# Linear-attention stack: one gelu group per pass on ScalarE, with feed-forward chunks 2 and 3 moved up on TensorE

## The chip, the cores and the metric

One NeuronCore of one Trainium2 chip runs the whole program. The metric is the device time of one execution in microseconds (us); lower is better. The engines work side by side and meet only at semaphores: TensorE (PE in the rows; PEld is its weight loads) multiplies matrices, VectorE (DVE) and ScalarE (ACT) work on tiles, GpSimd (POOL) does small work, and SyncE (SP) issues transfers. Each takes its instructions in the order in which they are written.

## The reference, cut to what matters

The program is a two-block network on 4096 tokens of width 128. The change touches only the attention of the second block, a stack of eight linear-attention layers with a feed-forward each:

```python
for i in range(8):
    residual = x
    Q = elu(einsum('nsd,hdk->nshk', x, Wq[i]) + bq[i]) + 1
    Kf = elu(einsum('nsd,hdk->nshk', x, Wk[i]) + bk[i]) + 1
    V = einsum('nsd,hdk->nshk', x, Wv[i]) + bv[i]
    KV, sumK = sum(Kf * V, axis=1), sum(Kf, axis=1)
    Z = 1.0 / (Q * sumK[:, None] + 1e-06)
    att = (Q * KV[:, None] * Z).reshape(n, s, H * K)
    y = gelu(att @ Wo[i] + bo[i])
    x = layer_norm(y + residual, ln1_s[i], ln1_b[i])
    residual = x
    h = gelu(x @ W1[i] + b1[i])
    h = gelu(h @ W2[i] + b2[i])
    x = layer_norm(h + residual, ln2_s[i], ln2_b[i])
```

There are 16 heads of 64, so Q, Kf and V have 1024 rows per token; the hidden width of the feed-forward is 512. Each layer therefore has three gelus. A unit of 512 tokens has six gelu instructions: one on y, four on the chunks of the hidden layer, and one on the second product.

## The kernel before, in words

The stack (`stack_phase`, L1378) cuts the tokens into eight units of 512 (two images of 256) and takes the 64 pairs of layer and unit one after the other. It is a software pipeline, unrolled by `run` (L1459): pass t does the first part of unit t, and later parts of units t-1 to t-4. In the code A, B, C, Dn and E say whether the unit with lag 0, 1, 2, 3 or 4 exists. From pass 4 to pass 63 all five do; from pass 3 on there is a unit with lag 3. Every engine has a `step` function that writes its part of a pass in a fixed order by hand, and the engines are joined by counting semaphores alone. Nothing reorders them.

What one pass does around the change:

- The 1024 rows of K, Q and V are made in four quarters of two 128-row chunks. `biases` (L1514) writes the bias rows of K and Q of a quarter into PSUM (it waits until VectorE has taken the quarter before: k_ready and q_ready). `keys`, `queries` and `values` (L1533 to L1545) then run three matmuls of 512 columns per chunk, because each weight and each input is split into a high and a low part. `values` makes one chunk at a time in a single bank, and waits until VectorE has drained the chunk before (v_drained).
- ScalarE takes exp of each quarter (`exp_keys` L1699, `exp_queries` L1703), VectorE makes the feature maps from it (`feature_k` L1826, `feature_q` L1865), and multiplies and sums keys with values (`values` L1837, "drain the values").
- For the unit with lag 1, ScalarE makes 1/(Q sumK) by a log (`log_z` L1707) and an exp (`exp_z` L1720); VectorE multiplies it in (`attention` L1872), quarter by quarter; and TensorE projects each quarter with Wo (`project` L1547), which waits for att_ready. Quarter 0 is done in the same pass as the quarter-0 and quarter-1 keys of the next unit.
- For the unit with lag 3, `first_feed_forward` (L1558) makes the four hidden chunks. They use two PSUM banks in turn: chunk 2 waits for the gelu of chunk 0 (hid_ready), chunk 3 for the gelu of chunk 1. `first_gelu` (L1688) takes them on ScalarE. `second_feed_forward` (L1570) sums them.
- `turn` (L1580) transposes a 128 x 512 tile by four small matmuls. The normalisations run on VectorE between two turns (`layernorm_stats` L1884, then GpSimd's `rstd_of`, then `normalise` L1893).

ScalarE's functions come in sets: gelu is in one, exp and log are together in another, and to change the set it runs an ACT_TABLE_LOAD. In a pass it now has two groups of gelus. The first has four: the second product's (L1749), chunk 0, y (L1754), chunk 1. Then come a load of the exp and log set (L1762), `exp_z` of quarter 0, and `exp_keys` and `exp_queries` of quarter 1; then a load of the gelu set, the gelus of chunks 2 and 3, and again a load of the exp and log set (L1777), before `log_z` of quarter 1. TensorE's order there is (L1618 to L1645, without the waits of a layer's first pass):

```python
first_feed_forward(t - 3, 1)
biases(t, 1)
values(t, s, 0, 0)
keys(t, s, 1)
queries(t, s, 1)
first_feed_forward(t - 3, 2)
values(t, s, 0, 1)
first_feed_forward(t - 3, 3)
project(t - 1, r, 0)
turn(m0, y2, c["z2_turned"])
values(t, s, 1, 0)
biases(t, 2)
queries(t, s, 2)
turn(m1, y1, c["z1_turned"])
keys(t, s, 2)
turn(m0, y2, c["n2_turned"])
```

VectorE's order between the drain of the last values chunk of unit t-1 and its second normalisation is: add y2 and x1; `finish_sums`; drain values (t, 0, 0); `attention` (t-1, 0); `feature_k` (t, 1); drain values (t, 0, 1); `feature_q` (t, 1); `layernorm_stats` of y2; add y1; drain values (t, 1, 0); `normalise` y2.

The last pass of a layer also moves the next layer's weights into place on ScalarE and VectorE (`swap`), and the first pass of the next layer the rest of them.

Of the kernel before, what the change touches and what calls it, by code (L numbers as in the profile page):

```python
# [1377 lines left out]
def stack_phase(nc, sem, d, g):  # L1378
# [10 lines left out]
    with ExitStack() as ctx:  # L1389
# [76 lines left out]
        def active(at, lag):  # L1466

            return 0 <= at - lag < UNITS
# [41 lines left out]
        def _(pe):  # L1510
# [13 lines left out]
            def three_pass(out, kind, chunk, s, first):  # L1524
                cols = slice(chunk * P, (chunk + 1) * P)
                pe.matmul(out, w_hi[:, kind, cols], x_hi[:, s, :], start=first, stop=False, skip_group_check=True)  # L1526
                pe.matmul(out, w_hi[:, kind, cols], x_lo[:, s, :], start=False, stop=False, skip_group_check=True)  # L1527
                return pe.matmul(out, w_lo[:, kind, cols], x_hi[:, s, :], start=False, stop=True, skip_group_check=True)  # L1528

            def weights_ready(u, piece):  # L1530
                pe.wait_ge(c["w_ready"], NS * layer_of(u) + place_of_swap[piece] + 2)

            def keys(t, s, q):  # L1533
                for half in range(2):
                    last = three_pass(k_ps[:, half * UNIT:(half + 1) * UNIT], 0, 2 * q + half, s, False)
                last.then_inc(c["k_filled"], 1)

            def queries(t, s, q):
                for half in range(2):
                    last = three_pass(q_ps[:, half * UNIT:(half + 1) * UNIT], 1, 2 * q + half, s, False)  # L1540
                last.then_inc(c["q_filled"], 1)

            def values(t, s, q, half):
                pe.wait_ge(c["v_drained"], 8 * t + 2 * q + half + 1)
                three_pass(v_ps[:], 2, 2 * q + half, s, True).then_inc(c["v_filled"], 1)  # L1545

            def project(u, s, q):  # L1547

                pe.wait_ge(c["att_ready"], 4 * u + q + 2)
                if q == 0:  # L1550
                    pe.wait_ge(c["y1_ready"], u + 1)
                pe.wait_ge(wo_in[q], 16 * layer_of(u) + 16)
                for chunk in (2 * q, 2 * q + 1):
                    last = pe.matmul(o_ps[:], wo[:, chunk, :], feat_q[:, s, chunk, :], start=(chunk == 0), stop=(chunk == NC - 1),  # L1554
                                     skip_group_check=True)
                last.then_inc(c["o_filled"], 1)

            def first_feed_forward(u, j):  # L1558

                bank, cols = (m1, m0)[j % 2], slice(j * P, (j + 1) * P)  # L1560
                if j == 0:
                    pe.wait_ge(c["x1_split"], u + 2)
                    pe.wait_ge(c["w1_ready"], layer_of(u) + 2)
                else:
                    pe.wait_ge(c["hid_ready"], 4 * u + max(j, 1))
                pe.matmul(bank[:], w1_hi[:, cols], x1_hi[:], start=True, stop=False)
                pe.matmul(bank[:], w1_hi[:, cols], x1_lo[:], start=False, stop=False)
                pe.matmul(bank[:], w1_lo[:, cols], x1_hi[:], start=False, stop=True).then_inc(c["w1_filled"], 1)
# [11 lines left out]
            def turn(bank, y, turned):  # L1580
                for i in range(4):
                    last = pe.transpose(bank[:, i * P:(i + 1) * P], y[:, i * P:(i + 1) * P], ident)  # L1582
                last.then_inc(turned, 1)

            def step(t, at, closing=None, opening=None, second=False):
                s, r = at % 2, 1 - at % 2
                A, B, C, Dn, E = (active(at, k) for k in range(5))
                opens = opening is not None or at == 0
                bias_step = 4 * layer_of(t) + 2
                if C:  # L1590
                    project(t - 2, s, 1)
                if Dn:
                    pe.wait_ge(c["n1_ready"], 4 * (t - 3) + 5)
                    turn(m1, y1, c["n1_turned"])
                if A:
                    if opens:
                        pe.wait_ge(c["b3_ready"], bias_step)
                    biases(t, 0)
                    pe.wait_ge(c["x_split"], t + 2)
                    if opens:  # L1600
                        weights_ready(t, (KEYS, 0))
                    queries(t, s, 0)
                    keys(t, s, 0)
                if B:
                    if second or at == 1:
                        weights_ready(t - 1, (VALUES, 3))
                    values(t - 1, r, 3, 0)
                if Dn:
                    first_feed_forward(t - 3, 0)
                if C:  # L1610
                    project(t - 2, s, 2)
                    project(t - 2, s, 3)
                if B:
                    values(t - 1, r, 3, 1)
                if Dn:
                    if E:
                        pe.wait_ge(c["y2_ready"], t - 4 + 2)
                    first_feed_forward(t - 3, 1)  # L1618
                if A:
                    if opens:  # L1620
                        pe.wait_ge(c["b3_ready"], bias_step + 1)
                    biases(t, 1)
                    if opens:
                        weights_ready(t, (VALUES, 0))
                    values(t, s, 0, 0)
                    keys(t, s, 1)
                    queries(t, s, 1)
                if Dn:
                    first_feed_forward(t - 3, 2)
                if A:  # L1630
                    values(t, s, 0, 1)
                if Dn:
                    first_feed_forward(t - 3, 3)
                if B:
                    project(t - 1, r, 0)
                if E:
                    pe.wait_ge(c["z2_ready"], t - 4 + 2)
                    if Dn:
                        pe.wait_ge(c["hid_ready"], 4 * (t - 3) + 5)
                    turn(m0, y2, c["z2_turned"])  # L1640
                if A:
                    if opens:
                        pe.wait_ge(c["b3_ready"], bias_step + 2)
                        weights_ready(t, (VALUES, 1))
# [3 lines that stand above are left out]
                if C:  # L1648
                    pe.wait_ge(c["z1_ready"], t - 2 + 2)
                    if Dn:  # L1650
                        pe.wait_ge(c["hid_ready"], 4 * (t - 3) + 4)
                    turn(m1, y1, c["z1_turned"])
                if A:
                    keys(t, s, 2)
                if E:
                    pe.wait_ge(c["n2_ready"], 4 * (t - 4) + 5)
                    turn(m0, y2, c["n2_turned"])
                if A:
                    values(t, s, 1, 1)
                if Dn:  # L1660
                    second_feed_forward(t - 3, E)
                if A:
                    if opens:
                        pe.wait_ge(c["b3_ready"], bias_step + 3)
                        weights_ready(t, (VALUES, 2))
                    values(t, s, 2, 0)
                    biases(t, 3)
                    keys(t, s, 3)
                    queries(t, s, 3)
                    values(t, s, 2, 1)  # L1670
# [4 lines left out]
        def _(act):  # L1675
            act.wait_ge(const_in, 32)

            def param(u, k):
                return params[:, bass.ds(layer_of(u), 1), k]
# [8 lines left out]
            def first_gelu(u, j):  # L1688

                act.wait_ge(c["w1_filled"], 4 * u + j + 2)  # L1690
                act.activation(hid[:, j, :], (m1, m0)[j % 2][:], ACT.Gelu_apprx_tanh, bias=param(u, 1 + j)).then_inc(c["hid_ready"], 1)
# [33 lines left out]
            def step(t, at, closing=None, opening=None, second=False):  # L1725
                s, r = at % 2, 1 - at % 2
                A, B, C, Dn, E = (active(at, k) for k in range(5))
# [30 lines left out]
                    swap(opening, VALUES, 3)  # L1758
                if Dn:
                    first_gelu(t - 3, 1)  # L1760
                if A or B:
                    act.preload_act_table_set("natural_log_exp_and_others")  # L1762
                if B:
# [4 lines left out]
                if closing is not None:  # L1768
# [1 line left out]
                    swap(closing, QUERIES, 1)  # L1770
                    act.wait_ge(c["v_filled"], 8 * t + 3)
                    swap(closing, VALUES, 0)
                if Dn:
                    first_gelu(t - 3, 2)
                    first_gelu(t - 3, 3)
                if A or B:
                    act.preload_act_table_set("natural_log_exp_and_others")  # L1777
                if B:
                    log_z(t - 1, r, 1)
                    exp_z(t - 1, 1)  # L1780
# [815 lines left out]
```

## Time and profile before

| What | us |
|---|---|
| Median of 3 runs | 3323.68 |
| Lowest and highest of them | 3323.03, 3341.3 |
| The profiled execution | 3324.58 |
| Its span in the trace | 3322.8 |
| The stack's steady stretch, 1000 to 3000 of the span | granted clock 1.00 |
| From one pass to the next, most passes | 35.1 |
| The last pass of a layer | 38.2 |

The span runs from the first to the last instruction in the trace, and the profiled execution's own time is 1.8 us more. Start times are counted from the start of the span. A row of the timeline gives the start, the busy time, the engine, the line, the operation with the tiles it writes and reads, how many like it are merged in the row, and in brackets how long its engine stood idle before it and which instruction ended the wait. The durations of matmuls overlap: they are pipelined, so that the pitch from start to start is what one costs. The granted clock is 1.00 at 2.4 GHz and 0.50 at 1.2 GHz.

### The profile page before, as it was taken

The numbers are of one execution on the slowest core, as the hardware profiler recorded it, in microseconds if no ns is written. First come the engines' busy times: TensorE is split into PE (matmuls) and PEld (weight loads), VectorE is DVE, ScalarE is ACT, GpSimd is POOL, SyncE is SP. The second block draws the span as 40 slices with busy tenths as digits, with TensorE's granted clock in tenths as the row PEclk, the third lists the DMA queues.
The fourth block names the chain that finished last, engine by engine and source line by source line (L and its number), as shares of the span: only waits on it lengthen the run. The fifth ranks groups of instructions, "written<-read, shape, count | busy, mean of one in ns | idle before, by whom it ended". The sixth has DMA issues, their size and how long they took to land. (4 is left out here: it accounts for less than half of the span.)

```text
span 3322.8 us, 49526 instructions
## 1 busy us (share of the span) xinstructions
PE 3011.6 (91%) x14486; PEld 1989.9 (60%) x14486; DVE 2777.8 (84%) x11011; ACT 2463.9 (74%) x4579; POOL 589.9 (18%) x715
## 2 busy tenths in 40 slices
PE   7999998282799999999999999999999999999779
PEld 5777776271566566566666656666665665666454
DVE  6878786864689999998999998999989999898566
ACT  6878786132578878878888888888888888878535
POOL 0000001276011111111111111111211111111124
PEclk9999998585999999999999999999999999999869
DMA  1000000323000000000000000000000000000000
GB/s 55 1 1 1 0 1 4 110 39 90 1 1 1 7 26 1 3 31 1 1 7 26 1 4 29 1 1 7 26 1 7 26 1 1 7 11 1 1 1 26
DMA packets 35120, 46.39 MB, mean 14 GB/s; under 512 B 5768, under 2 KB 26304, under 8 KB 34880
## 3 DMA queue, kind: packets, MB, share of 16 engines
q1 hardware_dynamic: 29248, 39.47, 3.6%
q0 software_dynamic: 5632, 4.20, 1.0%
q8 instruction: 93, 1.52, 0.2%
q14 instruction: 147, 1.20, 0.1%
HBM read 35.16 MB, written 8.49 MB: 13 GB/s over the span
## 5 line engine op out<-in xcount | busy, mean ns | idle before, releaser
L1880 DVE TENSOR_SCALAR t_feat_q<-t_recip,t_neg_mean 128x256 f32<-128x256 f32 x1024 | 385.5, 438 | 131.4 <-ACT t_recip L1723 131.4
L1554 PE MATMUL t_o_ps<-t_feat_q,t_wo 128*128 128x512 f32 x1024 | 473.0, 595 | 2.7 <-DVE t_feat_q L1880 2.7
L1715 ACT ACTIVATE t_recip<-t_feat_q,t_z_scale 128x256 f32<-128x256 f32 x1024 | 434.7, 498 | 3.5 <-DVE t_feat_q L1880 2.7
L1701 ACT ACTIVATE t_exp_k<-t_k_ps 128x1024 f32<-128x1024 f32 x256 | 259.4, 1013 | 230.2 <-PE t_k_ps L1528 230.2
L1843 DVE CUSTOM_DVE_ANT_0 t_junk<-t_v_ps,t_feat_k 128x256 f32<-128x256 f32 x1024 | 390.3, 418 | 6.1 <-PE t_v_ps L1528 6.0
L1833 DVE SCALAR_TENSOR_TENSOR t_feat_k<-t_exp_k,t_k_ps 128x256 f32<-128x256 f32 x1024 | 368.7, 415 | 21.4 <-ACT t_exp_k L1701 21.4
L1705 ACT ACTIVATE t_exp_q<-t_q_ps 128x1024 f32<-128x1024 f32 x256 | 261.7, 1022 | 96.8 <-PE t_q_ps L1528 94.5
L1869 DVE SCALAR_TENSOR_TENSOR t_feat_q<-t_exp_q,t_q_ps 128x1024 f32<-128x1024 f32 x256 | 312.5, 1221 | 8.8
L2008 POOL TENSOR_TENSOR t_var_eps<-t_moments,t_ln_eps 128x4 f32<-128x4 f32 x128 | 69.2, 540 | 1300.1 <-DVE t_moments L1891 1300.1
L1554 PEld LDWEIGHTS t_o_ps<-t_feat_q,t_wo 128*128 128x128 f32 x1024 | 194.3, 190 | 175.4 <-issue 154.5
L1526 PE MATMUL t_v_ps<-t_x_hi,t_w_hi 128*128 128x512 f32 x512 | 264.4, 516 | 10.1 <-DVE t_sum_kv L1843 9.3
L1723 ACT ACTIVATE t_recip<-t_recip 128x1024 f32<-128x1024 f32 x256 | 269.7, 1054 | 2.7
L1577 PE MATMUL t_m<-t_hid,t_w 128*128 128x512 f32 x512 | 241.1, 615 | 18.4 <-ACT state_t L1785 18.4
L1526 PE MATMUL t_q_ps<-t_x_hi,t_w_hi 128*128 128x512 f32 x512 | 218.1, 426 | 2.5 <-POOL t_x_lo L2015 2.5
L1526 PE MATMUL t_k_ps<-t_x_hi,t_w_hi 128*128 128x512 f32 x512 | 216.9, 424 | 0.0
L1582 PEld LDWEIGHTS t_m<-ident,t_y 128*128 128x128 f32 x1024 | 118.9, 142 | 150.6 <-issue 92.9
L1896 DVE TENSOR_SCALAR t_y<-t_m,t_moments,t_rstd 128x128 f32<-128x128 f32 x512 | 174.3, 400 | 36.4 <-POOL t_rstd L2010 36.4
L1528 PE MATMUL t_k_ps<-t_x_hi,t_w_lo 128*128 128x512 f32 x512 | 204.3, 399 | 0.0
L1528 PE MATMUL t_q_ps<-t_x_hi,t_w_lo 128*128 128x512 f32 x512 | 204.0, 398 | 0.0
L1527 PE MATMUL t_k_ps<-t_x_lo,t_w_hi 128*128 128x512 f32 x512 | 203.7, 398 | 0.0
L1527 PE MATMUL t_q_ps<-t_x_lo,t_w_hi 128*128 128x512 f32 x512 | 203.5, 397 | 0.0
L1527 PE MATMUL t_v_ps<-t_x_lo,t_w_hi 128*128 128x512 f32 x512 | 202.8, 396 | 0.0
(365 smaller groups left out, 7341.2 us busy)
## 6 DMA issues: line engine op xcount, KB each, us to landing
t_raw_w<-in_wq SPq DMA_DIRECT2D x8, 512.0 KB, 3.7
t_raw_w<-in_wk SPq DMA_DIRECT2D x8, 512.0 KB, 4.8
t_raw_w<-in_wv SPq DMA_DIRECT2D x8, 512.0 KB, 5.6
t_wo<-in_wo SPq DMA_DIRECT2D x32, 128.0 KB, 2.2
x<-in_x SPq DMA_DIRECT2D x4, 512.0 KB, 8.4
tokens_dram<-r_hn SPq DMA_DIRECT2D x8, 256.0 KB, 2.3
e_w_raw<-in_fc_w SPq DMA_DIRECT2D x4, 512.0 KB, 4.0
e_w<-in_fc_w SPq DMA_DIRECT2D x4, 512.0 KB, 4.9
```

The source lines that it names most:

```text
L1526: pe.matmul(out, w_hi[:, kind, cols], x_hi[:, s, :], start=first, stop=False, skip_group_check=True)
L1527: pe.matmul(out, w_hi[:, kind, cols], x_lo[:, s, :], start=False, stop=False, skip_group_check=True)
L1528: return pe.matmul(out, w_lo[:, kind, cols], x_hi[:, s, :], start=False, stop=True, skip_group_check=True)
L1554: last = pe.matmul(o_ps[:], wo[:, chunk, :], feat_q[:, s, chunk, :], start=(chunk == 0), stop=(chunk == NC - 1), skip_group_check=True)
L1701: act.activation(exp_k[:], k_ps[:], ACT.Exp, bias=-1.0).then_inc(c["k_exp"], 1)
L1705: act.activation(exp_q[:], q_ps[:], ACT.Exp, bias=-1.0).then_inc(c["q_exp"], 1)
L1715: last = act.activation(recip[:, q % 2, k * UNIT + n * SEQ:k * UNIT + (n + 1) * SEQ], feat_q[:, s, chunk, cols], ACT.Ln, bias=1.0, scale=z ...
L1723: act.activation(recip[:, q % 2, :], recip[:, q % 2, :], ACT.Exp, scale=-1.0).then_inc(c["recip_ready"], 1)
L1833: last = dve.scalar_tensor_tensor(feat_k[:, q % 2, cols], exp_k[:, cols], 1.0, k_ps[:, cols], ALU.min, ALU.max, accum_out=sum_k[:, s, n, 2 ...
L1843: last = dve.tensor_tensor_reduce(junk[:, n, :], v_ps[:, n * SEQ:(n + 1) * SEQ], feat_k[:, q % 2, k * UNIT + n * SEQ:k * UNIT + (n + 1) * ...
L1869: dve.scalar_tensor_tensor(feat_q[:, s, 2 * q:2 * q + 2, :], exp_q[:].rearrange("p (k t) -> p k t", k=2), 1.0, q_ps[:].rearrange("p (k t) ...
L1880: last = dve.tensor_scalar(feat_q[:, s, chunk, cols], recip[:, q % 2, k * UNIT + n * SEQ:k * UNIT + (n + 1) * SEQ], -1.0, neg_mean[:, s, n ...
```

## The change

On TensorE the order inside a pass becomes: values chunk 0, feed-forward chunk 2, keys of quarter 1, feed-forward chunk 3, queries of quarter 1, values chunk 1, projection of quarter 0. On ScalarE the gelus of chunks 2 and 3 follow that of chunk 1 at once, ahead of the load of the exp and log set; their former place, and the second load of that set, are gone. VectorE, GpSimd and SyncE keep their programs. All waits stay attached to the same instructions.

```diff
@@ TensorE's step
                     values(t, s, 0, 0)
-                    keys(t, s, 1)
-                    queries(t, s, 1)
                 if Dn:
                     first_feed_forward(t - 3, 2)
                 if A:
-                    values(t, s, 0, 1)
+                    keys(t, s, 1)
                 if Dn:
                     first_feed_forward(t - 3, 3)
+                if A:
+                    queries(t, s, 1)
+                    values(t, s, 0, 1)
                 if B:
                     project(t - 1, r, 0)
@@ ScalarE's step
                 if Dn:
                     first_gelu(t - 3, 1)
+                    first_gelu(t - 3, 2)
+                    first_gelu(t - 3, 3)
                 if A or B:
                     act.preload_act_table_set("natural_log_exp_and_others")
                 if B:
...
-                if Dn:
-                    first_gelu(t - 3, 2)
-                    first_gelu(t - 3, 3)
-                if A or B:
-                    act.preload_act_table_set("natural_log_exp_and_others")
                 if B:
                     log_z(t - 1, r, 1)
                     exp_z(t - 1, 1)
```

## Rows read from the trace of the kernel before

**Rows 1.** Part 1 of the page: busy us, share of span, instructions.

```profile
PE 3011.6 (91%) x14486; PEld 1989.9 (60%) x14486; DVE 2777.8 (84%) x11011; ACT 2463.9 (74%) x4579; POOL 589.9 (18%) x715
```

**Rows 2.** Windows view, one pass: busy us (instructions) per engine, granted clock, DMA.

```profile
1535.09:1570.20 35.11, 34.47 (x142) 21.93 (x141) 31.60 (x124) 29.27 (x42) 5.70 (x6) 1.00 0.00 1
```

**Rows 3.** Groups by line, ScalarE, 1000 to 3000: busy us, mean ns, idle.

```profile
L1777 ACT ACT_TABLE_LOAD x56 | 71.8, 1283 | 1.0
```

**Rows 4.** Timeline, TensorE, same pass: start, us, line, operation, count, wait before.

```profile
1537.15 0.50 PE L1526 MATMUL t_v_ps<-t_x_hi,t_w_hi 128*128 128x512 f32 x1
...
1537.95 0.40 PE L1526 MATMUL t_k_ps<-t_x_hi,t_w_hi 128*128 128x512 f32 x1
...
1539.36 0.40 PE L1526 MATMUL t_q_ps<-t_x_hi,t_w_hi 128*128 128x512 f32 x1
...
1540.75 0.40 PE L1566 MATMUL t_m<-t_x_hi,t_w_hi 128*128 128x512 f32 x1
...
1541.45 0.40 PE L1526 MATMUL t_v_ps<-t_x_hi,t_w_hi 128*128 128x512 f32 x1
...
1542.86 1.88 PE L1554 MATMUL t_o_ps<-t_feat_q,t_wo 128*128 128x512 f32 x4
1544.70 0.63 PE L1582 MATMUL t_m<-ident,t_y 128*128 128x128 f32 x4
...
1545.96 0.39 PE L1521 MATMUL t_k_ps<-t_ones_b,t_b 3*128 3x512 bf16 x2
...
1549.85 0.66 PE L1582 MATMUL t_m<-ident,t_y 128*128 128x128 f32 x4
```

**Rows 5.** Timeline of ScalarE in the same pass.

```profile
1536.93 0.69 ACT L1691 ACTIVATE t_hid<-t_m,t_params 128x512 f32<-128x512 f32 x1
...
1538.93 1.06 ACT L1723 ACTIVATE t_recip<-t_recip 128x1024 f32<-128x1024 f32 x1
1539.89 1.00 ACT L1701 ACTIVATE t_exp_k<-t_k_ps 128x1024 f32<-128x1024 f32 x1
1540.95 1.03 ACT L1705 ACTIVATE t_exp_q<-t_q_ps 128x1024 f32<-128x1024 f32 x1
1542.00 1.28 ACT L1691 ACT_TABLE_LOAD   x1
1543.29 1.26 ACT L1691 ACTIVATE t_hid<-t_m,t_params 128x512 f32<-128x512 f32 x2
1544.57 1.28 ACT L1777 ACT_TABLE_LOAD   x1
1545.87 1.71 ACT L1715 ACTIVATE t_recip<-t_feat_q,t_z_scale 128x256 f32<-128x256 f32 x4
```

**Rows 6.** Timeline of VectorE in the same pass.

```profile
1536.96 0.08 DVE L1843 DVE_READ_ACCUMULATOR2_ANT t_sum_kv<- 128x1 f32 x1
...
1540.09 1.14 DVE L1880 TENSOR_SCALAR t_feat_q<-t_recip,t_neg_mean 128x256 f32<-128x256 f32 x4 [0.97 <-ACT t_recip L1723]
1541.15 0.41 DVE L1833 SCALAR_TENSOR_TENSOR t_feat_k<-t_exp_k,t_k_ps 128x256 f32<-128x256 f32 x1
...
1543.92 1.22 DVE L1869 SCALAR_TENSOR_TENSOR t_feat_q<-t_exp_q,t_q_ps 128x1024 f32<-128x1024 f32 x1
1545.37 0.89 DVE L1887 BATCH_NORM_STATS2 t_stats<-t_m 128x6 f32<-128x128 f32 x4 [0.22 <-PE t_m L1582]
...
1548.43 1.36 DVE L1896 TENSOR_SCALAR t_y<-t_m,t_moments,t_rstd 128x128 f32<-128x128 f32 x4 [0.49 <-POOL t_rstd L2010]
```

**Rows 7.** Timeline of TensorE in pass 64, at project quarter 0.

```profile
3106.69 3.15 PE L1554 MATMUL t_o_ps<-t_feat_q,t_wo 128*128 128x512 f32 x4 [2.66 <-DVE t_feat_q L1880]
```

**Rows 8.** Windows view, columns as in rows 2, behind rows 7.

```profile
3107.00:3110.00 3.00, 3.00 (x6) 1.12 (x5) 0.00 (x0) 2.97 (x5) 0.00 (x0) 0.56 0.00 0
```

**Rows 9.** Timeline of TensorE in pass 11: its wait at the bias rows.

```profile
1206.93 0.39 PE L1521 MATMUL t_k_ps<-t_ones_b,t_b 3*128 3x512 bf16 x2 [1.42 <-DVE t_feat_q L1869]
```

**Rows 10.** Windows view, columns as in rows 2, around rows 9.

```profile
1205.00:1212.00 7.00, 5.58 (x29) 4.09 (x28) 5.97 (x16) 5.07 (x8) 1.33 (x1) 1.00 0.10 35
```

## The prediction

> **What bounds the kernel now.** I read the engines' totals first: TensorE is busy 91% of the span, VectorE 84%, ScalarE 74% [rows 1]. ScalarE, from which the change takes work, is the third engine. Then one pass of the stack by itself: of 35.11 us TensorE is busy for 34.47, VectorE for 31.60, ScalarE for 29.27, at full clock [rows 2]. So TensorE could gain at most 35.11 - 34.47 = 0.64 us in a pass, even if nothing made it wait. Then the three timelines of that same pass [rows 4 to 6], because the engines run fixed orders and what counts is who waits for whom. The place to look at is VectorE's attention of quarter 0 at 1540.09: it had waited 0.97 us for ScalarE's `exp_z` [rows 6], which ran at 1538.93, after the first gelu group and a table load [rows 5]. So ScalarE is late already at just this point, and the change puts two more gelus ahead of it.
>
> **The change, part by part.** All times below are those of the pass in rows 4 to 6; I start from the values of chunk 0 on TensorE at 1537.15, which cannot start sooner: the last values drain of the unit before ends at 1536.96 + 0.08 = 1537.04 [rows 6].
>
> *Removed on ScalarE:* one load of the gelu set and one of the exp and log set, 1.28 us each [rows 5]; the grouped view has the second at 1283 ns in the mean over 56 passes [rows 3]. That is 2.57 us of ScalarE's pass. Nobody gains it at once: the next instruction behind the loads is `log_z` of quarter 1 at 1545.87 [rows 5], whose result VectorE takes only after its second normalisation, which starts at 1548.43 [rows 6].
>
> The Trainium skill's page "ScalarE: Activation LUTs" (Table sets: the hidden batching unit, and What ACT_TABLE_LOAD costs) says to batch activations by set and prices a switch at about 2.66 us with its drain; two switches would be 5.3 us. Here the load at 1542.00 takes 1.28 and the gelu starts at 1543.29 [rows 5], so no drain shows, and the trace's price is used.
>
> *Moved on TensorE:* the matmuls are the same, 0.233 us from start to start: keys of quarter 1 start at 1537.95, queries at 1539.36, so six cost 1.40; feed-forward chunk 2 at 1540.75 and values at 1541.45, so three cost 0.70 [rows 4]. In the new order chunk 2 starts at 1537.95, the keys at 1538.65, chunk 3 at 1540.05; its last matmul starts 0.47 later and ends 0.40 after that, at 1540.92. Their own waits are met: chunk 2 needs the gelu of chunk 0, which precedes that of chunk 1 in the group; chunk 3 needs that of chunk 1, which ends at 1536.93 + 0.69 = 1537.62 [rows 5], well before 1540.05.
>
> *The wait that this adds on ScalarE:* the gelu of chunk 3 cannot start before 1540.92, plus the hand-over (from `exp_z`'s end to attention it is 0.10, 1539.99 to 1540.09 [rows 5, 6]; between nothing and that I take 0.04): 1540.96. Chunk 2's gelu goes in the gap before it. ScalarE stands idle for most of 1537.62 to 1540.96, and behind the waiting instruction are queued the table load, `exp_z` of quarter 0, and the exps of keys and queries of quarter 1. From the start of the last gelu of the group to the start of `exp_z` took 1538.93 - 1536.93 = 2.00, and from there to attention 1540.09 - 1538.93 = 1.16 [rows 5, 6]. So attention of quarter 0 starts at 1540.96 + 3.16 = 1544.12, which is 4.03 us later than now. The exps of keys and queries follow at 1543.92 and 1544.98, in time for VectorE's next steps.
>
> *Who waits for that, VectorE first.* Its order is fixed, so it idles for 5.0 us in place of 0.97. Then `feature_k`, a drain and `feature_q` run without waits as now, and `feature_q` ends 5.05 us after attention starts (1543.92 + 1.22 - 1540.09) [rows 6]: 1549.17. The statistics of y2 then start at once, and the 0.22 us that they wait for a transpose today [rows 6] are gone. The 0.49 us for GpSimd behind them stays, since nothing in that stretch changes. The second normalisation ends 1548.43 + 1.36 + 4.03 - 0.22 = 1553.60: 3.81 us late.
>
> *TensorE.* It reaches the projection of quarter 0 at 1542.86 as now [rows 4], but attention ends 1.06 after its start, so it waits until about 1545.25: a stall of 2.4 us. Projection (1.84) and transpose (0.4) bring it to 1547.5, values to 1548.3, and there the bias rows of quarter 2 wait for `feature_q` until 1549.25 (now 1545.96, 3.3 us late). Queries, transpose and keys follow; the transpose behind the second normalisation starts at 1553.65, against 1549.85 [rows 4]: **3.8 us late**.
>
> *Does anything get it back before the pass ends?* From that transpose to the next values of chunk 0 is 1537.15 + 35.11 - 1549.85 = 22.4 us, in which TensorE is busy but for some 0.6 us, and its work there doesn't change. ScalarE takes its work there from TensorE's results, so its 2.57 us don't help. VectorE is late by the same 3.8 and hands over in the same order. So a pass of 35.1 becomes 38.9.
>
> *The clock.* A stall of 2.4 us on TensorE is not in the steady passes of before. The nearest row is in pass 64, at the same instruction: after 2.66 us of waiting for attention, the two products of the projection took 3.15 us [rows 7] in place of 1.88 [rows 4], and the granted clock in the 3 us behind is 0.56 [rows 8], so mostly 1.2 GHz. A wait of 1.42 us in pass 11 left the clock at 1.00 [rows 9, 10]. So I expect the clock to fall in most passes. The price from below is 0: TensorE has some 1 us of waiting before the bias rows and 0.5 before the last transpose to absorb a late fall. From above: half of a low stretch of 3.4 us (3.0 us are shown [rows 8]), 1.7 us, if nothing absorbs it. If it falls right at the projection, that ends 1.27 later and the transpose (0.63) takes about 1 us, so y2's statistics start at some 1549.5 to 1549.6 in place of 1549.17: 0.4 us. I take 0.2, the middle of 0 and 0.4, since the fall in rows 8 is right behind the wait.
>
> *Count and sum.* The stall needs a unit with lag 3 and keys being made: passes 3 to 63, 61 of them. The passes at a layer's end hold the same steps, with weight copies behind `feature_q`; I take the same price. Passes 0 to 2 lose one idle table load each and pass 64 shifts by about a gelu either way; 0 for both, within 4 us. 61 x (3.8 + 0.2) = 244 us. The profiled execution took 3324.58, 0.9 above the median of the runs, so the sum gives 3568.6 against that one and **3568** against the median: 7% slower.
>
> **The rivals.**
> *Partly regained.* Once VectorE is 4 us behind, its other waits for ScalarE might vanish, since it would find the results lying ready: one or two waits of the size of attention's 0.97 us, 1.5 us in a pass. For it: ScalarE has 2.57 us less to do. Against it: those later results hang on matmuls that are late by as much. Then 3.8 - 1.5 = 2.3 a pass, 140 us: 3464.
> *The clock's price is not absorbed*, because the low stretch reaches into the 22.4 us where TensorE has no slack: 3.8 + 1.7 = 5.5 a pass, 335 us: 3659. For it: rows 7 and 8; against it: the 1.5 us of waits that lie right behind the stall.
> *No change.* VectorE is idle for 35.11 - 31.60 = 3.5 us in a pass [rows 2], near the 4.03 by which attention slips; if all of it could be moved there, 0.5 us times 61 at most: 3324 to 3354. Against it: that idle time is spread over waits that the order fixes. The Trainium skill's "Perfetto Trace Analysis" (Identifying the Most-Contended Engine) leads here too, by telling one to improve the busiest engine first: ScalarE is not that, so relief there would be worth nothing.
> *Faster.* The batching of the sets would win if ScalarE's lateness at attention were due to its load of work, so that 2.57 us less let `exp_z` come sooner. It decides at one point: `exp_z` of quarter 0 must start before 1538.93 of this pass. Then VectorE's 0.97 us go, TensorE falls to its busy time, and a pass gains 0.64: 61 x 0.64 = 39 us, 3285. Against it: by the diff `exp_z` is behind two more gelus, and the loads that go lie after it.
>
> **How the numbers follow.** Forecast, 3.4 to 4.6 us a pass (207 to 281 us, 3531 to 3604): 0.70. Partly regained: 0.12. Clock not absorbed: 0.11. No change: 0.04. Faster: 0.03. About 1% is what a measurement of this kernel can tell from none. Only the rival of that name is faster by over 1%, and only "no change" is within it; the others are slower: 0.03, 0.04, 0.93. The range takes in the forecast's own and about half of the two cases beside it: 3485 to 3630.
>
> **What would show it.** Right: in a pass of the changed kernel two table loads in place of four; ScalarE waiting for TensorE before the gelu of chunk 3, some 2 us; VectorE's wait for `exp_z` of quarter 0 near 5 us; TensorE's projection of quarter 0 waiting near 2.4 us for attention, its bias rows of quarter 2 near 1 us for `feature_q`; passes of 38.9 to 39.3; the clock at 0.50 for a stretch behind the projection. Wrong: passes near 35, `exp_z` starting earlier against the values of chunk 0 than 1.78 us, the wait at the projection absent, or longer waits elsewhere on TensorE than these.

## The result and the profile after

The changed kernel takes 3562.7 us (median of 4 runs, 3558.74 to 3565.28) against 3323.36 of the kernel before in the same call: ratio 1.0698, 95% interval 1.0663 to 1.0733. It is slower by 7%, 239 us; forecast were 244. The profiled execution took 3561.36 us, its span 3559.6.

Part 1 of the page of the changed kernel answers to [rows 1]:

```profile
PE 3081.5 (87%) x14486; PEld 2018.7 (57%) x14486; DVE 2776.0 (78%) x11011; ACT 2300.7 (65%) x4452; POOL 589.9 (17%) x715
```

ScalarE has 163 us less to do, as was meant: 2463.9 before, 2300.7 now, and 127 instructions fewer. TensorE and VectorE have the same counts of instructions, VectorE the same busy time, and their shares of a longer span fell. TensorE's busy time rose by some 70 us with the same instructions; a part of that is a lower clock (below). So no engine got more work. Of the 237 us of span that came on top, TensorE stands idle in some 167, VectorE in all.

One pass, from one load of the exp and log set to the next, and a stretch of 3.5 us inside it, in the windows view of the changed kernel; columns as in [rows 2], the granted clock is the third figure from the end:

```profile
1646.48:1685.33 38.85, 35.96 (x141) 22.79 (x140) 31.56 (x123) 26.64 (x39) 5.71 (x6) 0.96 0.00 1
1651.00:1654.50 3.50, 3.50 (x10) 1.97 (x8) 3.47 (x13) 2.30 (x5) 0.00 (x0) 0.53 0.00 0
```

A pass takes 38.85 in place of 35.11, and in the stretch, which begins 0.86 us after the end of the stall and holds the rest of the projection, the granted clock is 0.53, near the lower of its two levels (1.2 GHz of 2.4). Over 48 passes, from pass 8 to pass 56, the mean from load to load rose from 35.66 to 39.48. Now the same pass by timeline. It stands for the pass of rows 4 to 6, though it is one pass later in the run; values chunk 0 starts at 1641.98, where it was at 1537.15, so that 104.83 is to be taken off to compare. TensorE first; answering to [rows 4]:

```profile
1641.98 0.50 PE L1526 MATMUL t_v_ps<-t_x_hi,t_w_hi 128*128 128x512 f32 x1
...
1642.79 0.40 PE L1566 MATMUL t_m<-t_x_hi,t_w_hi 128*128 128x512 f32 x1
...
1643.48 0.39 PE L1526 MATMUL t_k_ps<-t_x_hi,t_w_hi 128*128 128x512 f32 x1
...
1644.88 0.40 PE L1566 MATMUL t_m<-t_x_hi,t_w_hi 128*128 128x512 f32 x1
...
1650.14 2.75 PE L1554 MATMUL t_o_ps<-t_feat_q,t_wo 128*128 128x512 f32 x4 [2.30 <-DVE t_feat_q L1878]
1652.68 1.06 PE L1582 MATMUL t_m<-ident,t_y 128*128 128x128 f32 x4
...
1654.83 0.39 PE L1521 MATMUL t_k_ps<-t_ones_b,t_b 3*128 3x512 bf16 x2
...
1658.51 0.60 PE L1582 MATMUL t_m<-ident,t_y 128*128 128x128 f32 x4
```

The reader sees the new order (values, chunk 2, keys, chunk 3), and then the stall: the projection of quarter 0 waits 2.30 us for attention. The two products take 2.75 in place of 1.88, the transpose behind them 1.06 in place of 0.63.

ScalarE, answering to [rows 5]:

```profile
1641.76 0.69 ACT L1692 ACTIVATE t_hid<-t_m,t_params 128x512 f32<-128x512 f32 x1
1643.68 0.69 ACT L1692 ACTIVATE t_hid<-t_m,t_params 128x512 f32<-128x512 f32 x1 [1.23 <-PE t_m L1568]
1645.78 0.69 ACT L1692 ACTIVATE t_hid<-t_m,t_params 128x512 f32<-128x512 f32 x1 [1.41 <-PE t_m L1568]
1646.48 1.28 ACT L1765 ACT_TABLE_LOAD   x1
1647.78 1.06 ACT L1724 ACTIVATE t_recip<-t_recip 128x1024 f32<-128x1024 f32 x1
1648.74 1.00 ACT L1702 ACTIVATE t_exp_k<-t_k_ps 128x1024 f32<-128x1024 f32 x1
1649.64 1.02 ACT L1706 ACTIVATE t_exp_q<-t_q_ps 128x1024 f32<-128x1024 f32 x1
1650.55 1.70 ACT L1716 ACTIVATE t_recip<-t_feat_q,t_z_scale 128x256 f32<-128x256 f32 x4
```

The gelu of chunk 2 waits 1.23 us for TensorE, the gelu of chunk 3 another 1.41. Only then come the load, `exp_z` of quarter 0 and the two exps. `log_z` follows with no load before it.

VectorE, answering to [rows 6]:

```profile
1648.94 1.14 DVE L1878 TENSOR_SCALAR t_feat_q<-t_recip,t_neg_mean 128x256 f32<-128x256 f32 x4 [4.99 <-ACT t_recip L1724]
1650.00 0.41 DVE L1831 SCALAR_TENSOR_TENSOR t_feat_k<-t_exp_k,t_k_ps 128x256 f32<-128x256 f32 x1
...
1652.78 1.22 DVE L1867 SCALAR_TENSOR_TENSOR t_feat_q<-t_exp_q,t_q_ps 128x1024 f32<-128x1024 f32 x1
1653.91 0.88 DVE L1885 BATCH_NORM_STATS2 t_stats<-t_m 128x6 f32<-128x128 f32 x4
...
1656.97 1.36 DVE L1894 TENSOR_SCALAR t_y<-t_m,t_moments,t_rstd 128x128 f32<-128x128 f32 x4 [0.49 <-POOL t_rstd L2008]
```

Attention waits 4.99 us for `exp_z`, where it was 0.97. The statistics of y2 no longer wait; the normalisation still waits 0.49 for GpSimd.

### The profile page after: what moved, and what is told of

Read it like the earlier page. It is cut to its first block and busy times, and to the rows that moved or that the text cites. A ratio compares the mean times of both kernels' runs of the same rounds, so it can differ in the third digit from the quotient of the medians.

```text
span 3559.6 us, 49399 instructions
## 1 busy us (share of the span) xinstructions
PE 3081.5 (87%) x14486; PEld 2018.7 (57%) x14486; DVE 2776.0 (78%) x11011; ACT 2300.7 (65%) x4452; POOL 589.9 (17%) x715
## 5 line engine op out<-in xcount | busy, mean ns | idle before, releaser
L1554 PE MATMUL t_o_ps<-t_feat_q,t_wo 128*128 128x512 f32 x1024 | 529.6, 654 | 144.9 <-DVE t_feat_q L1878 144.9
L1692 ACT ACTIVATE t_hid<-t_m,t_params 128x512 f32<-128x512 f32 x256 | 175.7, 686 | 164.3 <-PE t_m L1568 164.0
L1582 PEld LDWEIGHTS t_m<-ident,t_y 128*128 128x128 f32 x1024 | 133.3, 151 | 156.1 <-issue 88.6
L1528 PE MATMUL t_k_ps<-t_x_hi,t_w_lo 128*128 128x512 f32 x512 | 205.0, 400 | 0.0
L1528 PE MATMUL t_q_ps<-t_x_hi,t_w_lo 128*128 128x512 f32 x512 | 203.7, 398 | 0.0
```

## The experiments

All are cut from one of the two kernels. "Pass" is the time from one load ahead of `exp_z` to the next in a plain pass of the profile (not a layer's last, first or fourth); the kernel before has 35.10, and 34.92 in a layer's second pass.

| Run | us | Ratio to before, 95% | Pass |
|---|---|---|---|
| the changed kernel | 3562.7 | 1.0698 (1.0663 to 1.0733) | 38.80 to 39.19 |
| gelus_only | 3716.35 | 1.118 (1.1155 to 1.1204) | 40.95 to 42.1 |
| order_only | 3407.28 | 1.025 (1.0227 to 1.0272) | 36.48 |
| fill_stall | 3551.96 | 1.0689 (1.0671 to 1.0707) | 38.80 |
| gelus_only_fill | 3678.51 | 1.1066 (1.1044 to 1.1089) | 40.91 |
| load_back | 3556.52 | 1.0707 (1.0689 to 1.0725) | 38.80 to 39.2 |
| chunks_early | 3465.59 | 1.043 (1.0409 to 1.0451) | 37.40 |
| chunks_first | 3414.21 | 1.0283 (1.0261 to 1.0305) | 36.52 |
| exp_z_ahead | 3561.87 | 1.0715 (1.0691 to 1.0738) | 38.48 to 39.4, three of 40.8 to 40.9 |
| exp_z_ahead_before | 3371.34 | 1.0138 (1.0118 to 1.0159) | 35.93 |
| chunks_early_exp_z_ahead | 3441.26 | 1.0357 (1.0336 to 1.0377) | 37.08 |
| exp_z_ahead_bias_first | 3338.51 | 1.0043 (1.0027 to 1.006) | 35.40 |

**Each half alone.** gelus_only is the changed kernel with TensorE's old order:

```diff
                     values(t, s, 0, 0)
-                if Dn:
-                    first_feed_forward(t - 3, 2)
-                if A:
                     keys(t, s, 1)
+                    queries(t, s, 1)
                 if Dn:
-                    first_feed_forward(t - 3, 3)
+                    first_feed_forward(t - 3, 2)
                 if A:
-                    queries(t, s, 1)
                     values(t, s, 0, 1)
+                if Dn:
+                    first_feed_forward(t - 3, 3)
```

> The six gelus in one group on ScalarE, TensorE's order as before. My theory (the group's last gelu waits for feed-forward chunk 3, and exp_z of quarter 0 stands behind it): chunk 3 ends at 1543.02 of the worked pass in place of 1540.92, so attention slips by 6.1 us and the pass by 5.9: about 61 x 5.9 = 360 us over before, 3685, slower than the changed kernel by some 120. Rival (TensorE's new order makes the loss, and the gelus by themselves do no harm): within 1% of before, 3323. Rival (the group itself costs a fixed amount wherever the chunks are): as the changed kernel, 3563.

It is worse than the whole change, so the group of gelus makes the loss and TensorE's new order takes part of it back. The shortest passes are 40.95, that is 5.85 over before, where 5.9 was expected. The median lies 31 us above my sum; where these come from is shown with the fillers below.

order_only is the kernel before with only the edit of TensorE's step in the diff above.

> TensorE's new order, ScalarE's order as before with two gelu groups and four table loads. My theory: the queries of quarter 1 are ready 1.4 us later, so their exp, the second group and the transpose that waits for its last gelu slip by about 1.2 us; nothing else: 61 x 1.15 = 70 us, about 3393. Rival (TensorE's new order makes the whole loss): 3563. Rival (the order is harmless): 3323.

The direction and the place were right: the waits of TensorE in this run, 1000 to 3000 of the span (us in total, times, longest), begin with the transpose that waits for the last gelu, in all 54 passes:

```profile
PE t_m L1582 <- ACT t_hid L1692: 80.3, 54, 2.3
```

That is some 1.4 us in a plain pass (36.48 against 35.10), a bit more than the 1.15 I gave.

**Where chunk 3 stands.** chunks_early is the changed kernel with chunk 2 behind chunk 1, and chunk 3 behind the first values chunk:

```diff
                     first_feed_forward(t - 3, 1)
+                    first_feed_forward(t - 3, 2)
...
                     values(t, s, 0, 0)
                 if Dn:
-                    first_feed_forward(t - 3, 2)
+                    first_feed_forward(t - 3, 3)
                 if A:
                     keys(t, s, 1)
-                if Dn:
-                    first_feed_forward(t - 3, 3)
```

chunks_first has both behind chunk 1:

```diff
                     first_feed_forward(t - 3, 1)
+                    first_feed_forward(t - 3, 2)
+                    first_feed_forward(t - 3, 3)
...
                     values(t, s, 0, 0)
-                if Dn:
-                    first_feed_forward(t - 3, 2)
                 if A:
                     keys(t, s, 1)
-                if Dn:
-                    first_feed_forward(t - 3, 3)
```

> The changed kernel with feed-forward chunk 2 directly behind chunk 1 and chunk 3 directly behind the first values chunk, ahead of the keys of quarter 1. My theory (the start of the last gelu sets the pass): chunk 3 ends 1.4 us sooner, at 1539.52 of the worked pass, attention at 1542.72, 2.6 later than before; a pass of 37.5, 61 x 2.4 = 147 us over before, about 3471. Rival (the loss is fixed by the group's six gelus on ScalarE): 3563. Rival (moving chunks ahead of keys only moves the delay to the keys): 3563 or more.

> The changed kernel with feed-forward chunks 2 and 3 directly behind chunk 1, ahead of the bias rows, values and keys. My theory (the start of the group's last gelu sets the pass): chunk 3 now waits for the gelu of chunk 1 and ends at 1538.57 of the worked pass, its gelu starts at 1538.6, attention at 1541.76, 1.7 later than before; a pass of 36.5, 61 x 1.45 = 88 us over before, about 3411, with no stall at the projection and the clock at 1.00. Rival (values and keys, now 1.6 us later on TensorE, become the bound): as with the chunks early, 3466, or more.

Both came within 6 us. With the same six gelus in one group on ScalarE, four places of chunk 3 on TensorE give four times: the longer the last gelu waits, the longer the pass. In chunks_first VectorE's waits for `exp_z` (up to three in a pass; 1000 to 3000) are back near the 114.5 us that the kernel before had in that list, and the clock in the windows view is at 1.00:

```profile
DVE t_feat_q L1874 <- ACT t_recip L1720: 114.1, 142, 1.1
DVE t_junk L1837 <- PE t_v_ps L1528: 87.6, 58, 1.8
```

```profile
1000.00:3000.00 2000.00, 1873.85 (x7537) 1180.52 (x7535) 1745.45 (x6741) 1467.45 (x2185) 323.80 (x344) 1.00 0.03 9
```

The second row is a wait that the list of the kernel before does not have. The values now stand behind both chunks on TensorE, so VectorE waits for values chunk 0 and only then for `exp_z` (1.61 and 1.04 us in the pass whose attention starts at 1640.18). So the first row does not mean that `exp_z` comes as early as before: it still ends last ahead of attention. What is left in this run, 1.4 us a pass, I put down to the gelus of chunks 2 and 3, which still run ahead of `exp_z` and the exps of quarter 1; the later values were not tried by themselves.

**The loads.** load_back puts one load back, in front of `log_z` of quarter 1:

```diff
+                if A or B:
+                    act.preload_act_table_set("natural_log_exp_and_others")
                 if B:
                     log_z(t - 1, r, 1)
```

> The changed kernel with one needless load of the exp and log set put back before log_z of quarter 1 (1.28 us of ScalarE in every pass). My theory (the loads that went lay off the path; log_z has over 2 us of room): no change, within 0.2% of 3563. Rival (the loads saved give something back that hides a larger loss): 61 x 1.28 = 78 us more, 3641.

No change: the intervals of the two ratios overlap. The timeline of ScalarE in this run shows why: with the load back, ScalarE still waits 1.42 us for the queries of quarter 2 (L1528).

```profile
1646.93 1.28 ACT L1777 ACT_TABLE_LOAD   x1
1648.23 1.71 ACT L1716 ACTIVATE t_recip<-t_feat_q,t_z_scale 128x256 f32<-128x256 f32 x4
1649.97 1.06 ACT L1724 ACTIVATE t_recip<-t_recip 128x1024 f32<-128x1024 f32 x1
1652.44 1.02 ACT L1706 ACTIVATE t_exp_q<-t_q_ps 128x1024 f32<-128x1024 f32 x1 [1.42 <-PE t_q_ps L1528]
```

In a pass of the changed kernel at the same granted clock (1607.69 to 1646.48, 1.00), the same wait is 2.83 us:

```profile
1617.37 1.03 ACT L1706 ACTIVATE t_exp_q<-t_q_ps 128x1024 f32<-128x1024 f32 x1 [2.83 <-PE t_q_ps L1528]
```

So this load is worth nothing where it was taken out: its 1.28 us a pass went into that wait. The other load, of the gelu set, was not put back.

**The clock.** fill_stall puts nine matmuls in TensorE's stall, gelus_only_fill eighteen in the longer one of gelus_only; their result is overwritten by the projection:

```diff
                     values(t, s, 0, 1)
+                if A and Dn:
+                    pe.wait_ge(c["y1_ready"], t)
+                    for _ in range(9):
+                        pe.matmul(o_ps[:], w1_hi[:, 0:P], x1_hi[:], start=True, stop=True)
                 if B:
                     project(t - 1, r, 0)
```

> The changed kernel with nine matmuls of 512 columns into the projection's free bank, in TensorE's stall before the projection of quarter 0 (2.1 us of the 2.3; their result is overwritten). The clock should stay at 1.00 there. My theory (the waits behind the stall absorb most of a low clock): 0 to 0.4 us a pass less, 0 to 24 us: 3539 to 3563. Rival (the low clock is a good part of the loss): 1.5 us a pass less, some 90 us: 3470. If the nine don't fit the stall, up to 0.3 us a pass more.

> The six gelus in one group with TensorE's order as before, and 18 matmuls of 512 columns (4.2 us, their result is overwritten) in its stall of 4.4 us before the projection. This asks for what the first run of that order lost beyond my sum. Theory (it was the low clock behind the longer stall): the steady pass is 40.96 throughout, and the time falls by some 35 us from 3716, to about 3681. Rival (the sum missed a wait): no change, 3716.

The windows view over 1000 to 3000, first of the changed kernel (granted clock 0.97), then of fill_stall (1.00):

```profile
1000.00:3000.00 2000.00, 1807.13 (x7095) 1132.81 (x7091) 1636.43 (x6328) 1374.18 (x2053) 302.23 (x321) 0.97 0.03 9
```

```profile
1000.00:3000.00 2000.00, 1873.02 (x7576) 1198.49 (x7575) 1642.31 (x6355) 1377.74 (x2061) 304.74 (x324) 1.00 0.03 9
```

With the filler plain passes are 38.80 throughout, where the changed kernel has 38.80 to 39.19; the means over 48 passes are 39.33 and 39.48, so the low clock costs about 0.15 a pass, some 9 us in all. The medians differ by 10.7, but the intervals of the ratios overlap, so the time alone doesn't show it. The profiled execution of fill_stall was the longest of its four (3566.05, the others 3551 to 3552), but the excess lies behind the stack: from its last load to the end of the span are 235 us, against 222 in the changed kernel. From the first load to the last it is 10 us shorter than the changed kernel (2494.6 against 2504.8). In gelus_only the stall is 4.4 us. Its windows over one such stall and as long behind it show the clock at 1.00 and then 0.61:

```profile
1649.00:1653.40 4.40, 0.02 (x1) 0.00 (x0) 1.18 (x5) 4.32 (x5) 0.00 (x0) 1.00 0.00 0
1653.40:1657.80 4.40, 4.39 (x11) 2.58 (x11) 4.37 (x17) 3.18 (x6) 0.00 (x0) 0.61 0.00 0
```

There the filler takes 38 us off, with intervals far apart, and all plain passes go to 40.9: the low clock covers the 31 us of the first miss.

**exp_z ahead of the group.** Three runs move `exp_z` of quarter 0 behind `exp_keys` of quarter 0, ahead of the gelus: exp_z_ahead on the changed kernel, chunks_early_exp_z_ahead on chunks_early, exp_z_ahead_before on the kernel before:

```diff
                 if A:
                     exp_keys(t, 0)
+                if B:
+                    exp_z(t - 1, 0)
...
-                if B:
-                    exp_z(t - 1, 0)
                 if A:
                     exp_keys(t, 1)
```

> The changed kernel with exp_z of quarter 0 moved ahead of the gelu group, behind exp_keys of quarter 0. My theory: attention no longer waits (5.0 us gone on VectorE, 2.3 us gone on TensorE at the projection), but the exps of keys and queries of quarter 1 still stand behind the last gelu, so feature_k starts 2.9 us later than before in place of 4.0: a pass of 37.7, 61 x 2.6 = 160 us over before, about 3485. Rival (exp_z's lateness is the whole loss): back to 3323. Rival (TensorE's stall at the projection and its clock are the loss): also back near 3323 with the clock at 1.00.

> The kernel before with exp_z of quarter 0 ahead of its first gelu group. VectorE's wait of 0.97 us at attention goes. My theory (TensorE bounds the pass, and no wait of TensorE hangs on this one): no change within 0.3%, 3318 to 3326. Rival (ScalarE's lateness at attention is on the path already before the change): 61 x 0.64 = 39 us less at most, 3285.

> Both repairs: chunks 2 and 3 early, and exp_z of quarter 0 ahead of the group. My theory: the exp of the keys of quarter 1 starts at 1541.55 of the worked pass and feature_k at 1542.6, 1.45 later than before; a pass of 36.3, 61 x 1.2 = 75 us over before, about 3400. Rival (the two repairs act on the same wait and don't add): as the better of the two alone, 3471 to 3485.

All three were slower than expected, by 77, 48 and 41 us. On the kernel before, attention's wait was gone and the pass yet 0.83 longer. The list of TensorE's waits in exp_z_ahead_before shows what took its place:

```profile
PE t_m L1566 <- ACT t_y L1751: 36.7, 53, 1.2
```

Feed-forward chunk 1 waits for the gelu of the second product, whose PSUM bank it takes over. That gelu starts the group, and moving `exp_z` ahead of it moved it back by 1 us. My sum had looked at who waits for `exp_z` and not at who waits for the group's first gelu. exp_z_ahead_bias_first is exp_z_ahead_before, and lets TensorE make the bias rows of quarter 1 in that wait (shown without the waits of a layer's first pass):

```diff
-                if Dn:
-                    if E:
-                        pe.wait_ge(c["y2_ready"], t - 4 + 2)
-                    first_feed_forward(t - 3, 1)
                 if A:
                     biases(t, 1)
+                if Dn:
+                    if E:
+                        pe.wait_ge(c["y2_ready"], t - 4 + 2)
+                    first_feed_forward(t - 3, 1)
+                if A:
                     values(t, s, 0, 0)
```

> The kernel before with exp_z of quarter 0 ahead of its first gelu group, as in exp_z_ahead_before, and with the bias rows of quarter 1 ahead of feed-forward chunk 1 on TensorE. This asks why exp_z_ahead_before lost 0.83 us a pass, which my sum had not. Theory (chunk 1 waits for the gelu of the second product, which now ends 1.0 us later; they share a bank): the bias rows fill 0.4 of that wait, values of chunk 0 start 0.35 later than in the kernel before in place of 0.83: passes of 35.45, about 3345. Rival (exp_z's own new place costs, whoever waits on TensorE): no change against 3371. Rival (bias rows first cost something of their own): over 3371.

3338.51 and a pass of 35.40: chunk 1's wait falls from 36.7 us to 5.8 in the same stretch, and a smaller one for the keys' feature map comes up.

```profile
PE t_k_ps L1521 <- DVE t_feat_k L1834: 10.7, 49, 0.2
...
PE t_m L1566 <- ACT t_y L1752: 5.8, 14, 0.6
```

So filling the missed wait gave back 0.53 of the 0.83; the other 0.3 were not tried apart. The wait itself is 0.7 us a pass in each of the three runs (36.7 us over 53 times, 34.8 over 50 in exp_z_ahead, 37.8 over 54 in chunks_early_exp_z_ahead), or some 43 us over 61 passes, close to the misses of 48 and 41. In exp_z_ahead it is one of three:

```profile
PE t_k_ps L1521 <- DVE t_feat_q L1867: 77.5, 102, 1.5
PE t_v_ps L1526 <- DVE t_sum_kv L1841: 53.5, 51, 1.1
PE t_m L1566 <- ACT t_y L1752: 34.8, 50, 1.2
```

Most of the rest of that run's 77 us goes with the clock, as the windows view shows pass by pass. There are 37 plain passes between pass 4 and pass 62. Of these 19 have a granted clock of 1.00 and take 38.46 to 38.50; 15 have 0.96 and take 39.33 to 39.44; three have 0.92 and take 40.8 to 40.9. Two neighbours:

```profile
1603.47:1641.94 38.47, 34.86 (x141) 21.95 (x140) 31.55 (x123) 26.55 (x40) 5.69 (x6) 1.00 0.00 1
1641.94:1681.36 39.42, 36.23 (x141) 23.26 (x140) 31.94 (x123) 26.55 (x39) 5.88 (x6) 0.96 0.00 1
```

In both, TensorE's two waits of 1.04 and 0.98 us are the same; only what follows them takes longer in the second. The mean of the 37 is 39.05, so the low clock costs 0.57 a pass, an estimate of 35 us over 61 passes. No filler was tried here.

No version beats the kernel before. The nearest, exp_z_ahead_bias_first, is slower by 0.27 to 0.6%, and it keeps two gelu groups.

## Why the prediction was right

Point by point, with times counted from the start of values chunk 0 of the same pass:

- *What bounds the pass.* That the load ahead of `log_z` lies off the path held: load_back gave the same time. Whether TensorE had 0.64 us to gain, no run shows. The Trainium skill's "ScalarE: Activation LUTs" (Table sets: the hidden batching unit) advises to batch by set; here the batch was made, saved what the trace priced, and lost 7%.
- *The wait added on ScalarE.* `exp_z` was forecast 5.81 us after values chunk 0 (1542.96 less 1537.15) and came after 5.80 (1647.78 less 1641.98); before it was 1.78. Two waits showed where I had named the second alone; the first, for chunk 2, was "the gap before it".
- *VectorE.* Attention forecast at 6.97, measured 6.96; its wait 5.0, measured 4.99. The 0.22 at the statistics went, as said.
- *TensorE.* The stall at the projection was forecast 2.4, measured 2.30; the transpose behind the second normalisation 16.50 after values chunk 0, measured 16.53. The wait at the bias rows, forecast near 1 us, is absent from the pass shown: the low clock had used it up. In the pass before it (1607.69 to 1646.48), at a granted clock of 1.00, it is 0.88:

```profile
1615.34 0.39 PE L1521 MATMUL t_k_ps<-t_ones_b,t_b 3*128 3x512 bf16 x2 [0.88 <-DVE t_feat_q L1867]
```

  In fill_stall, at a granted clock of 1.00, TensorE's waits for `feature_q` sum to 75.4 us against 48.0 in the changed kernel.
- *Nothing regained.* Nearly so. Mean of 48 passes: 39.48 - 35.66 = 3.82. Of these the clock is 0.15, the rest 3.67, against 3.8 forecast for a plain pass. Plain passes at full clock are 38.80 against 35.10, so 3.70. In the pass shown the transpose behind the second normalisation is 3.83 late, but the next values chunk 0 only 3.74, so some 0.1 us was regained in the stretch in which the forecast allowed for nothing.
- *The clock.* It fell in most passes: of the plain passes between pass 4 and pass 62, 14 have a granted clock of 1.00 and take 38.77 to 38.81, and 23 have 0.96 and take 38.79 to 39.19, 39.02 in the mean. So a pass in which it fell costs 0 to 0.4, 0.22 in the mean, where the forecast had 0 to 0.4 and took 0.2 for every pass; over all passes it is 0.15, because it does not fall in each. The rival in which it is not absorbed was wrong: 0.15 in place of 1.7 a pass here, and 0.4 even in gelus_only, whose stall is 2 us longer.
- *The count.* From the first load to the last the stack took 234 us longer in the two profiled executions, 3.84 if put on 61 passes; the other 3 us of the 237 us of span lie outside it. The forecast of 244 was 61 times 4.0: the pass was put 0.1 too long and the clock 0.05, some 9 us together, and the 3 us outside came on top.

The rivals fell as follows: "partly regained" by the sum above; "no change" by VectorE's 5 us wait in every pass; "faster" because `exp_z` came 4 us later, not sooner. And exp_z_ahead_before shows that, moved ahead of the group as it stands, `exp_z` gains nothing, though VectorE's 0.97 us go.

## What to carry to other kernels

Where engines run fixed orders, an instruction pulled ahead on one engine brings its wait with it, and everything behind it on that engine waits too: price the instructions that it is moved past, by who needs them, before pricing what it saves. Look at both ends of a moved group: who waits for its last member (here attention, through `exp_z`), and who waits for its first (chunk 1, through its bank), since in exp_z_ahead_before, where a whole group moved back by 1 us, the pass grew by 0.83 that the first reading had missed. And take relief on an engine at nothing unless a wait for that engine, on the engine that sets the pass, ends sooner by it.

## What was not expected of the hardware

A stall twice as long cost more than twice as much by the clock: 2.3 us of idle TensorE cost 0.15 us a pass, 4.4 us cost 0.4 (41.82 against 41.43, mean of 48 passes, without and with the filler). The windows view by pass shows how. In the changed kernel 23 of the 37 plain passes have a granted clock of 0.96, the others 1.00. In gelus_only none has 1.00: 23 have 0.96, as the second row here, and 14 have 0.92, as the first:

```profile
1607.92:1649.76 41.84, 36.85 (x140) 23.20 (x140) 31.62 (x123) 26.66 (x39) 5.71 (x6) 0.92 0.00 1
1649.76:1690.72 40.96, 35.97 (x140) 22.83 (x140) 31.55 (x123) 26.66 (x39) 5.69 (x6) 0.96 0.00 1
```

A pass at 0.96 costs about the same in both, 0.22 and 0.24 on the average over a pass at full clock (38.80; 40.91 with the filler); one at 0.92 costs 0.94. So the longer stall costs more because the clock falls in more passes and stays low for longer in some. What lies behind the fall counts too: in exp_z_ahead a pass at the same 0.96 costs 0.92 (39.40 against 38.48). There the fall comes behind TensorE's two waits of 1 us; in the changed kernel waits for `feature_q` (0.88 in the pass at full clock) lie behind it and shrink. That these waits make the difference was not tried by itself.

Waits of 0.9 us, two in a pass, left the granted clock at 1.00: TensorE in chunks_early, at the projection and at the bias rows:

```profile
1618.24 1.98 PE L1554 MATMUL t_o_ps<-t_feat_q,t_wo 128*128 128x512 f32 x4 [0.90 <-DVE t_feat_q L1876]
...
1622.25 0.39 PE L1521 MATMUL t_k_ps<-t_ones_b,t_b 3*128 3x512 bf16 x2 [0.88 <-DVE t_feat_q L1865]
```

The two waits stand in the brackets. In the windows view of that run the clock over 1000 to 3000 is 1.00, so what chunks_early loses, 2.3 us in a plain pass, is not the clock. But waits of about 1 us are not always free of it: two of them, close together, stand ahead of the fall in exp_z_ahead, whose clock fell in 18 of 37 plain passes:

```profile
1646.49 0.50 PE L1526 MATMUL t_v_ps<-t_x_hi,t_w_hi 128*128 128x512 f32 x1 [1.04 <-DVE t_sum_kv L1841]
...
1648.44 0.39 PE L1521 MATMUL t_k_ps<-t_ones_b,t_b 3*128 3x512 bf16 x2 [0.98 <-DVE t_feat_q L1867]
```
